# Two-layer Mamba/attention model with routed experts: plain loads of x, down weights asked for one at a time, the routing table and picks of the last pair moved, and layer 0's gate/up weights asked for by ScalarE's queue

## The reference, cut to what matters

```
x = L0_attn_u                      # (16, 256, 256), float32
xn = layernorm(x)
x = x + mamba(xn) + moe0(xn)       # scan over a state of 64, 4 heads
xn = layernorm(x)
x = x + attention(xn) + moe1(xn)   # causal, 16 heads of 16

moe(xn):                           # 8 experts, every token goes to its best 2
    w, i = top_k(softmax(xn @ gate_w), 2);  w = w / sum(w)
    shared = (silu(xn @ sg) * (xn @ su)) @ sd
    routed = sum over the 2 picks of w * (silu(xn @ wg[i]) * (xn @ wu[i])) @ wd[i]
```

## Time and profile before

| | |
|---|---|
| three executions | 1408.76, 1407.96, 1412.47 us (median 1408.76) |
| profiled execution, its own time | 1414.86 us |
| its span, first to last instruction | 1413.0 us |
| mean granted TensorE clock | 0.985 of full speed |
| busy: PE / DVE / POOL / ACT | 1318.1 / 911.1 / 653.3 / 511.3 us |

### The profile page before, as it was taken

The page is one execution under the profiler, slowest core; times in us unless marked ns, Lnnn a source line. Parts: engine busy times, 40 slices in busy tenths (PEclk is TensorE's granted clock), DMA queues, the critical chain, the costliest instruction groups (busy, mean ns, idle before and its releaser), DMA issues.

```text
span 1413.0 us, 30111 instructions
## 1 busy us (share of the span) xinstructions
PE 1318.1 (93%) x10668; PEld 1039.2 (74%) x10684; DVE 911.1 (64%) x3115; ACT 511.3 (36%) x1096; POOL 653.3 (46%) x801
## 2 busy tenths in 40 slices
PE   7899999999999999899999889999998978999985
PEld 6788889888888888766766556666665647888874
DVE  4566534555556655499998788888888753333356
ACT  2122122222222222333333355565565634444431
POOL 2356423333333332455554144545544454677772
PEclk9999999999999999999999899999999999999998
DMA  9922951111111114600000111010110001233376
GB/s 340 222 43 31 75 100 59 46 46 46 51 48 46 46 49 158 187 1 0 0 0 0 53 39 47 24 47 24 47 46 9 10 2 54 94 103 102 129 228 233
DMA packets 77446, 102.05 MB, mean 72 GB/s; under 512 B 13021, under 2 KB 65260, under 8 KB 77312
## 3 DMA queue, kind: packets, MB, share of 16 engines
q1 hardware_dynamic: 59200, 62.35, 17.0%
q0 software_dynamic: 18112, 37.93, 8.3%
HBM read 64.26 MB, written 35.98 MB: 71 GB/s over the span
## 4 chain that ended last, share of the span: by engine, by line
PE 73%; DVE 11%; issue 7%; POOL 6%; DMA 1%; ACT 1%; another core or an unknown queue 0%; SPq 0%; DVEq 0%; POOLq 0%
PE score L1891 42%; PE mixed L1891 16%; PE side L1891 9%; DVE score L1729 4%; POOL y_rows L847 2%; PE side L2135 2%; POOL sh_dn L839 1%; PE side L1901 1%; POOL XN L839 1%; DVE ARENA L1737 1%; PE mixed L2345 1%; DVE WGU L1729 1%; POOL ARENA L812 1%; DVE X L1848 1%; POOL lists L777 1%
## 5 line engine op out<-in xcount | busy, mean ns | idle before, releaser
L839 POOL DMA_INDIRECT XN<-xn_rows,slot_tok x106 | 108.2, 1021 | 217.8 <-PE side L2135 191.3
L1729 DVE CUSTOM_DVE_ANT_0 score<-score,future_b 128x128 f32<-128x128 f32 (+1 forms) x512 | 167.3, 389 | 42.1 <-PE score L1891 41.5
L847 POOL DMA_INDIRECT y_rows<-sh_gu,slot_row x144 | 144.4, 1003 | 89.5 <-ACT sh_gu L1040 50.6
L875 POOL TENSOR_SCALAR_AFFINE_SELECT ARENA<-ARENA 128x256 f32<-128x256 f32 x256 | 102.7, 424 | 158.3 <-ACT ARENA L1080 158.1
L1891 PE MATMUL score<-xT,HT 128*128 128x128 f32 x912 | 167.2, 275 | 0.0
L1080 ACT ACTIVATE ARENA<-score 128x768 f32<-128x768 f32 x128 | 103.9, 811 | 136.8 <-PE score L1891 136.5
L1891 PE MATMUL score<-ARENA 32*128 32x256 f32 (+1 forms) x2048 | 127.3, 354 | 25.6 <-DVE WGU L1729 14.6
L777 POOL DMA_INDIRECT lists<-token_no,w_in x128 | 125.3, 979 | 34.5 <-issue 30.2
L1891 PEld LDWEIGHTS score<-xT,HT 128*128 128x128 f32 x912 | 134.0, 192 | 0.0
L812 POOL TENSOR_TENSOR ARENA<-tri_le,DT 128x1024 bf16<-128x1024 bf16 x48 | 90.2, 1894 | 88.8 <-PE mixed L1891 35.7
L1040 ACT ACTIVATE sh_gu<-mixed 128x256 f32<-128x256 f32 x144 | 55.2, 383 | 207.9 <-PE mixed L1891 207.9
(11 more groups left out here) (309 smaller groups left out, 2810.8 us busy)
## 6 DMA issues: line engine op xcount, KB each, us to landing
WGU<-in_gu SPq DMA_DIRECT2D x8, 1024.0 KB, 14.8
WGU<-y_rows SPq DMA_DIRECT2D x32, 256.0 KB, 3.1
ARENA<-y_rows SPq DMA_DIRECT2D x32, 256.0 KB, 3.9
xn_rows<-XN SPq DMA_DIRECT2D x24, 256.0 KB
X<-in_u SPq DMA_DIRECT2D x16, 256.0 KB, 8.5
ARENA<-in_dn SPq DMA_DIRECT2D x8, 512.0 KB
x_parked<-X SPq DMA_DIRECT2D x4, 1024.0 KB
X<-x_parked SPq DMA_DIRECT2D x4, 1024.0 KB
```

Of the source, the lines that this page charges most:

```text
L839: x["got"][j % ring].mark(eng.indirect_dma_start(XG[j % ring], None, xn_rows[l], bass.IndirectOffsetOnAxis(slot_tok[:, col:col + 1], 0)))
L847: x["out"][j % YRING[l]].mark(eng.indirect_dma_start(y_rows[g], bass.IndirectOffsetOnAxis(slot_row[:, col:col + 1], 0), yo(l, j), None))
L875: ins = eng.affine_select(out=m, in_=m, compare_op=ALU.is_ge, fill=0.0, base=0, pattern=[[0, 2], [1, P]], channel_multiplier=-1)
L1729: ins = eng.tensor_tensor_reduce(s, s, future, -1.0, BIG, ALU.add, ALU.min, NM[:, c, j, at:at + 1])
```

## The change

Five edits. (1) SP asks for x plainly six sequences ahead. (2) The seven down loads no longer follow each other at n = 1: one is asked for after each of the stores 1 to 7. (3) The eight gate/up loads leave SP's list; ScalarE issues one at the end of each of the eight turns in which s is 0 to 7. (4) In the last turns of attention, the second pick of the last pair goes from the end of turn 16 into turn 17, behind the first maxima and the shift; the ranking on PE goes behind `turn_out`; `table_index(2)` goes from turn 17 to turn 18; and the shared gate/up matmuls of sequence 0 in layer 1 with their SiLU go from turn 19 into turn 18, in two parts. (5) In turn 2, `turn_maxima(b, 0)` goes behind the next block of scores.

```diff
--- before.py
+++ after.py
@@ -626,22 +626,19 @@
         for l in range(2):
             eng.dma_start(lists[l].rearrange("(p n) o -> p (n o)", p=P), itmp_rows).then_inc(s_zero, 16)
         load_x(5)
-        for e in range(E):
-            eng.dma_start(wgu0[:, e, :, :], a["gu0"][e].rearrange("(k p) n -> p k n", p=P)).then_inc(s_wgu0, 16)
-
         def load_down(e):
             eng.dma_start(wdn0[:, e, :, :], a["dn0"][e].rearrange("(c p) n -> p c n", p=P)).then_inc(s_wdn0, 16)
         rows0 = xn_rows[0].rearrange("(t p) d -> p t d", p=P)
         for n in range(NSEQ):
-            for ahead in range(n + (6 if n < 2 else 8), min(n + (7 if n < 1 else 9), NSEQ)):
-                load_x(ahead)
+            if n + 6 < NSEQ:
+                load_x(n + 6)
             N[0]["xn"].wait(eng, n)
             v = n % len(XN0)
             N[0]["stored"][v].mark(eng.dma_start(rows0[:, n * CH:(n + 1) * CH, :], XN0[v]))
             if n == 1:
                 eng.wait_ge(s_zero, 32)
-                for e in range(E - 1):
-                    load_down(e)
+            if 0 < n < E:
+                load_down(n - 1)
         N[0]["tr"].wait(eng, NSEQ - 1)
         for v in (2, 3):
             N[0]["stored"][v].wait(eng, NSEQ // len(XN0) - 1)
@@ -931,9 +928,9 @@
             if a and a.v == 1:
                 logits_copy(0, a.i)
 
-        def ffn_silu(l, r, late=False):
+        def ffn_silu(l, r, late=False, parts=None):
             f, ni = FF[l], FF[l]["ni"]
-            for i in range(ni):
+            for i in parts or range(ni):
                 n = r.n * ni + i
                 f["gu"].wait(eng, n)
                 f["ht"].wait(eng, n, 2)
@@ -955,6 +952,8 @@
                 front(k)
             for k in fronts[1:]:
                 pair_copy(k)
+            if s and s.n < E:
+                eng.dma_start(wgu0[:, s.n, :, :], a["gu0"][s.n].rearrange("(k p) n -> p k n", p=P)).then_inc(s_wgu0, 16)
 
         def exp2(l):
             eng.wait_ge(s_m21, l + 1)
@@ -1108,8 +1107,6 @@
             if d:
                 exps(d, 1, 1)
                 exps(d, 2, 0)
-            if o and not d:
-                ffn_silu(1, of(0))
             if o:
                 o_copy(o)
             if o and not d:
@@ -1136,8 +1133,12 @@
                 k_copies(a, 0)
             if b:
                 exps(b, 0, 1)
+            if d and not b:
+                ffn_silu(1, of(0), True, [0])
             if d:
                 mixed_copy(d, 1)
+            if d and not b:
+                ffn_silu(1, of(0), True, [1])
             if a:
                 q_copies(a, 1)
             if b:
@@ -1758,8 +1759,10 @@
                 maxima(b, 0, 0)
             if d:
                 shift(d, 1)
-            if a and b and b.v == 1:
+            if b and b.v == 1:
                 pick_experts(1, b.i, [1])
+            if d and not b:
+                table_index(2)
             if a and a.n == SPLIT + 1:
                 table_row(1)
                 next_lists()
@@ -1775,11 +1778,9 @@
                 combine(c, [1])
             if b:
                 maxima(b, 1, 1)
-            if b and not a:
-                table_index(2)
             if o and not d:
                 for i in range(FF[1]["ni"]):
-                    gate_product(1, of(0), i)
+                    gate_product(1, of(0), i, True)
                 add_down(1, of(0))
             if o:
                 add_out(o)
@@ -1813,8 +1814,6 @@
                 maxima(b, 3, 1)
             if d:
                 normalise(d)
-            if a and a.n == NSEQ - 1:
-                pick_experts(1, a.i, [1])
             if a and a.n == SPLIT:
                 table_starts(1)
             if a and a.n == SPLIT + 1:
@@ -1943,11 +1942,11 @@
                 ins = eng.transpose(part.bank[0:BLOCK, at:at + m], block_f[0:m, :], ident[0:m, 0:m])
             ins.then_inc(s_turned, 1)
 
-        def ffn_up(l, r, late=None):
+        def ffn_up(l, r, late=None, parts=None):
             f, ni = FF[l], FF[l]["ni"]
             gu = sh_gu if l == 0 else sh_gu1
             tok = bass.ds(r.n * SEQ, SEQ)
-            for i in range(ni):
+            for i in parts or range(ni):
                 n = r.n * ni + i
                 if l == 0:
                     f["ht"].wait(eng, n, 4)
@@ -2355,21 +2354,18 @@
                 if b:
                     A["kc"].wait(eng, 2 * b.n + 1)
                 turn_maxima(d, 1)
-            if b and not a:
-                A["qc"].wait(eng, 2 * b.n + 1)
-                rank_tokens(1, NSEQ // 2 - 1)
-            elif b:
+            if b and a:
                 values(b, 0)
             if d:
                 A["vc"].wait(eng, d.n)
                 A["on"].wait(eng, d.n, 1)
                 weigh(d, 0)
             scores(1, now(0), held(2))
-            if o and not d:
-                eng.wait_ge(s_l1b, 16 * (3 + 2 * E + 1))
-                ffn_up(1, of(0))
             if o:
                 turn_out(o, d)
+            if b and not a:
+                A["qc"].wait(eng, 2 * b.n + 1)
+                rank_tokens(1, NSEQ // 2 - 1)
             if o and not d:
                 ffn_down(1, of(0))
             if b and a:
@@ -2391,11 +2387,12 @@
                     norm_stage(1, a)
             if o:
                 project_out(o, 1)
-            if b:
-                if d:
-                    A["oc"].wait(eng, 2 * d.n)
+            if b and d:
+                A["oc"].wait(eng, 2 * d.n)
                 turn_maxima(b, 0)
             scores(0, now(2), held(3))
+            if b and not d:
+                turn_maxima(b, 0)
             if a:
                 if a.v == 0 and not is_first(a):
                     N[1]["xT"].wait(eng, a.n)
@@ -2418,11 +2415,17 @@
             scores(0, now(3), now(0))
             if a:
                 queries(a, 1)
+            if d and not b:
+                eng.wait_ge(s_l1b, 16 * (3 + 2 * E + 1))
+                A["exp"][0].wait(eng, NSEQ * GROUPS - 1)
+                ffn_up(1, of(0), "last turn", [0])
             if d:
                 weigh(d, 3)
             scores(1, now(3), now(1))
             if a:
                 keys(a, 1)
+            if d and not b:
+                ffn_up(1, of(0), "last turn", [1])
             if d:
                 turn_mixed(d)
         eng.wait_ge(s_fill, 5)
```

## The result

The changed kernel took 1423.1 us (median of four executions, 1422.58 to 1424.58) where the kernel before took 1408.36 us beside it: a ratio of 1.0097, interval 1.0073 to 1.0120. It is slower by 1%. The forecast was 1394.9 us with a range up to 1402.

A forecast was written before the change was run, and what follows sets the result against it. PE, busy for 1318.1 of 1413.0 us, was taken as the bound, with its idle and slow-clock stretches to gain. The terms 5.6 + 3.0 + 5.3 = 13.9 us bring 1408.76 to 1394.9 us, range 1391 to 1402.

The forecast's parts named there:

- The start: First stage: earlier store of sequence 2 ends PE's 3.95 us stall and slow-clock work; 5.6 us gained, bounds 4.0 and 7.0.
- What is late next is nothing in this stage until the list: First stage, after the start: PE is busy from turn to turn, so no further wait before the list.
- leaves about 12 us for each: First stage: one gate/up load per turn has about 12 us to land; a lone megabyte took 6.2 us.
- Turn 2: Attention turn 2: next scores fill PE's 2.76 us gap and the clock stays up; 3.0 us gained, bounds 1.0 and 3.6.
- The last turns: Attention turns 17 to 19: pick, table and gate/up leave the chain, POOL takes back 1.5 us; 5.3 us gained, bounds 3.2 and 6.5.
- The list: End of the first stage: the list's fetch at about 186 us, with PE's wait for the turned list near 1.5 us.
- The one on the slower side: Rival, chance 0.03: each ScalarE issue holds it until the megabyte lands; 1413 us, a loss above 5.6 us an issue.
- no change: Rival, chance 0.05: traffic keeps sequence 2's store late, the 3.95 us stall stays, POOL takes back 5.3 us; about 1406 us.

The follow-up runs named there:

- four cells of queue and hour: Gate/up loads by SP or ScalarE, early or late: SP early 0.9951, SP late 1.0115, ScalarE early 0.9889, against the kernel before; ScalarE late is the changed kernel.
- before_again: The kernel before, unchanged, run once for its trace on the chips of the experiments, where the kernel before took 1491 to 1499 us.
- early_only: Edits (1), (2) and (3) alone on the kernel before, with the old attention; ratio 1.0053 (0.9998 to 1.0108).

## Why the prediction was wrong

**The start.** The term of 5.6 us was right as far as it went: 6.8 us were gained by 69 us, inside the bounds of 4.0 and 7.0. The eight issues on ScalarE took 0.37 to 0.46 us each and not the 0.97 that I took, and no wait of PE is seen behind them. The step that failed is the next one: "What is late next is nothing in this stage until the list", with the time for a block that "leaves about 12 us for each". It took the rate of a transfer from the earlier trace rows, which come from the first 40 us, for one that holds at any hour. Five of the eight blocks were asked for at 51 us and later, beside the scatters, where a packet takes nearly four times as long on average. They kept the engines busy up to the stall, and the store of sequence 8 took some 60 us. 24.2 us were lost for 6.8 gained. A warning stood in my own rows: the DMA engines are busy with a share of 1.06 while they move 67 GB/s. I read the share and passed over the rate beside it. It was no full warning, though. Where the last blocks went, the DMA engines of the kernel before were mostly idle:

```profile
80.00:100.00 20.00, 20.00 (x123) 17.21 (x122) 13.20 (x62) 4.37 (x10) 13.32 (x14) 1.00 0.21 40
```

A share of 0.21 for 40 GB/s is 190 GB/s per busy time, and the changed kernel moved 112 GB/s there at a share of 1.08.

The Trainium skill, DMA: Bandwidth & Descriptors, "Issuing engines are not separate DMA queues", says that transfers interleave on the same 16 DMA engines whichever engine started them. That agrees with the four cells of queue and hour, where the hour decides. My sentence on it, that only the spread could give the gain, should have asked what the spread would cost.

**Turn 2.** Of 3.0 us, 1.0 came, the lower bound. The gap shrank as worked out, but not the fall of the clock: 0.50 from 815 us on. The projections ran at the lower clock in every profiled kernel with the edit (3.74 to 3.78 us). On the other chips the turn took 25.9 us in before_again and 26.8 in early_only, both without the edit, and 25.7 to 26.1 us in the kernels with it. A gain of 1 us there is neither shown nor excluded.

**The last turns.** 5.3 us predicted, 5.4 us measured. The order of things was not quite the one I gave: POOL bound for 0.32 us only and not for 1.5, and the clock still fell for a while (1.32 and 1.39 us for two blocks of scores). The two misses roughly cancel, so that the close agreement is in part luck. (The upper bound of this term should have been 5.3 + 1.5 = 6.8 us, not 6.5.) On the other chips these turns took 56.4 us in before_again and 54.6 in early_only, and 46.1 to 46.5 us in the eleven kernels with the edits and the scatters in place, a gain of 8 to 10 us.

**The list.** The fetch was at 202.92 us, not 186, late by the stall; PE did not wait for the turned list at all.

**The rivals.** The one on the slower side blamed ScalarE's issues, and the threshold I gave, 5.6 us an issue, was never near. I had no rival in which the moved bytes themselves are slow. The case "no change" came closest in words, since it had the traffic make the store late, but it placed the harm at the first store and not at the ninth.

## What to carry to other kernels

Before a transfer is moved to another hour, read share and GB/s together in the window it moves to: busy engines that move little say that each byte may cost several times its usual price there (here 586 ns a packet instead of 158). Idle engines do not say the opposite, as the window from 80 to 100 us shows; a run in which the neighbour is moved away does. Then ask which small store queues up with it, and who needs that store's buffer. And a change that is two halves should be run as two halves: here the good one hid how bad the other was.

## What was not expected of the hardware

While POOL's indirect 4-byte writes ran, at 3% of the DMA engines' time, the packets of the 4 KB loads took 586 ns on average instead of 158 (195 in the same window without the scatters), because one in five took over 1 us, and stores of 256 KB took 55.4 and some 60 us instead of at most 5.9. Why these writes slow the others was not tried.

The same kernel took 1408 us on one chip and 1491 to 1499 us on others, and the latter show waits of several microseconds behind ScalarE that the first does not have. Most of the difference lies in the last stage: of the 73.7 us between the spans of before_again and before, 57.8 come after the first tile of layer 1, where PE waits 45.2 us in all for the products behind ScalarE's SiLU (DVE's line 1416) and not at all on the first chip. Their cause stays open.
